# A fused four-block kernel: new order of products and turnings in a projection, and a choice by quarters in a routing

## The reference, cut to what matters

```
h = shift_token(x)                      # x: 2 x 1024 x 128
q, k, v = split(h @ wqkv)               # each 2 x 1024 x 512
q = l2norm(q) * q_scale; k = l2norm(k) * k_scale
q, k = rotary_xpos(q, k)                # cos, sin and a scale by position
o = local_attention(q, k, v)            # windows of 64, looking one window back
x = x + o @ wo                          # then a gated feed-forward
```

```
s = softmax(x @ Wr + br)                # 2048 x 64
fs = where(mask(s), s, 0)               # mask: the best 512 groups of 64 sorted scores
fs = fs / (fs.sum(-1) + 1e-6)
h = silu(x @ Wup + bup) * (x @ Wgate + bgate) * fs
out = h @ Wdown + fs @ bdown
```

## Time and profile before

| what | value |
|---|---|
| time of the runs | 1203.18, 1209.27 and 1210.47 us; median 1209.27 |
| profiled execution | 1206.43 us, span of its instructions 1204.6 us |
| mean granted TensorE clock | 0.968 of full speed |
| busy in the span | PE 1074.0 us (89%), PEld 711.9 (59%), DVE 857.7 (71%), ACT 617.3 (51%), POOL 516.7 (43%) |
| POOL's two operations in the projection | 32 adds of 2364 ns mean, 32 multiplies of 1902 ns |

### The profile page before, as it was taken

One profiled execution on the slowest core, in us unless ns is written; L12 is line 12 of the kernel. 1 busy time (PEld: TensorE's weight loads), 2 busy tenths in 40 slices (PEclk: granted clock), 3 DMA queues, 4 the chain that ended last, 5 costly groups with the idle time before them and its releaser, 6 DMA issues. The chain is left out here.

```text
span 1204.6 us, 29628 instructions
## 1 busy us (share of the span) xinstructions
PE 1074.0 (89%) x11763; PEld 711.9 (59%) x11763; DVE 857.7 (71%) x1539; ACT 617.3 (51%) x1416; POOL 516.7 (43%) x453
## 2 busy tenths in 40 slices
PE   6799999899998879998888999876998999988998
PEld 4588655688553448655446856533665454444897
DVE  5788567787567978544886835797467589998655
ACT  3566455666445669544668924500664357754000
POOL 1476302667207985322996521033344047742200
PEclk9899999999999989999998999999999989988999
DMA  3200000200002210011220000000000011100011
GB/s 85 82 1 2 8 7 18 82 1 2 1 1 62 61 31 3 2 72 35 55 59 7 3 15 15 13 4 4 4 5 3 15 25 18 18 14 1 14 30 53
DMA packets 52791, 28.08 MB, mean 23 GB/s; under 512 B 35474, under 2 KB 46268, under 8 KB 52284
## 3 DMA queue, kind: packets, MB, share of 16 engines
q1 hardware_dynamic: 52668, 26.36, 8.8%
HBM read 17.17 MB, written 1.05 MB: 15 GB/s over the span
## 5 line engine op out<-in xcount | busy, mean ns | idle before, releaser
L363 POOL TENSOR_TENSOR A_pr<-A_pr,A_rs 128x1024 f32<-128x1024 f32 x64 | 121.1, 1894 | 57.0 <-DVE A_rs L430 57.0
L467 ACT ACTIVATE A_pr<-psb,A_nm 128x1024 f32<-128x1024 f32 x64 | 71.1, 1111 | 49.9 <-DVE A_nm L424 49.6
L420 DVE TENSOR_REDUCE A_mx<-psb 128x1 f32<-128x1024 f32 x64 | 78.1, 1220 | 8.3 <-PE psb L376 4.5
L1280 POOL TENSOR_TENSOR F_raw<-F_raw,F_rc 128x1024 f32<-128x1024 f32 x32 | 75.6, 2364 | 16.5 <-DVE F_raw L1350 16.0
L2116 PE MATMUL psb<-M_wd,M_gates 128*128 128x128 f32 x512 | 70.7, 282 | 0.0
L2050 PE MATMUL psb<-XL,M_wu 128*128 128x512 f32 x128 | 69.3, 624 | 1.2 <-ACT M_ST L2174 1.2
L2116 PEld LDWEIGHTS psb<-M_wd,M_gates 128*128 128x128 f32 x512 | 65.6, 195 | 3.9 <-DVE M_gates L2348 2.1
L2053 PE MATMUL psb<-XL,M_wg 128*128 128x512 f32 x128 | 67.5, 609 | 0.0
L2348 DVE TENSOR_TENSOR M_gates<-M_hall,psb 128x512 f32<-128x512 f32 x64 | 43.9, 687 | 33.1 <-PE psb L2111 33.0
L1298 PE MATMUL psb<-F_wqkv,F_hst 128*128 128x512 f32 x128 | 61.3, 601 | 6.2 <-ACT F_hst L1361 4.5
L389 PE MATMUL psb<-ident,A_pr 128*128 128x128 f32 x512 | 66.6, 285 | 0.0
(11 more groups left out here) (396 smaller groups left out, 2974.8 us busy)
## 6 DMA issues: line engine op xcount, KB each, us to landing
F_VS<-F_V SPq DMA_DIRECT2D x62, 128.0 KB, 2.3
F_raw<-in_c_xpos_dram SPq DMA_DIRECT2D x3, 1024.0 KB, 4.8
F_wqkv<-in_L_ffn_wqkv_dram SPq DMA_DIRECT2D x3, 768.0 KB, 7.3
A_w<-in_L_attn_w_dram SPq DMA_DIRECT2D x4, 256.0 KB, 3.6
M_wu<-in_L_ffn_Wup_dram SPq DMA_DIRECT2D x16, 64.0 KB, 2.0
M_wg<-in_L_ffn_Wgate_dram SPq DMA_DIRECT2D x16, 64.0 KB, 2.1
M_wd<-in_L_ffn_Wdown_dram SPq DMA_DIRECT2D x16, 64.0 KB, 1.7
M_sel<-in_c_select_dram SPq DMA_DIRECT2D x16, 64.0 KB, 1.9
```

The source lines that it names most:

```text
L363: pool.tensor_tensor(p, p, rs[:, u % 2:u % 2 + 1].broadcast_to([P, SEQ]), ALU.mult).then_inc(scaled, 1)
L420: dve.tensor_reduce(mx[:, u % 2:u % 2 + 1], sview(u), AX, ALU.max).then_inc(maxed, 1)
L467: act.activation(pr[:, u % NP, :], sview(u), ACT.Exp, bias=nm[:, u % 2:u % 2 + 1], scale=scale, accum_out=su[:, u % 2:u % 2 + 1]).then_inc ...
L1280: pool.tensor_tensor(rs[:, o, :], rs[:, o, :], rc[:, o, :], ALU.add).then_inc(unit, 1)
```

## The change

In the projection `make` is cut in two. It now ends after the query and key products and signals a new semaphore, `paired`; the value product becomes a step `value` of its own, with its wait for `v_kept` and its signal `made`. The order on PE becomes `make(n)`, `turn(n - 3)`, `value(n)`, and one turning is left over after the loop. ACT squares when `paired` comes, then keeps the queries and keys of tile `n - 3`, and only then waits for `made` and keeps the value. DVE's wait for POOL moves from before the sum to behind it. In the routing the choice is written in quarters, one ahead of the remainder that needs it; ACT's rounding waits for its own quarter; and POOL's last four gatings wait for all four remainders.

```diff
@@ -1246,8 +1246,8 @@
-                    g = (loaded, zeroed, staged, made, squared, v_kept, summed, rooted, inv, roped, unit, turned, q_kept, k_kept,
-                         dstep, v_moved) = sems("F1", "loaded zeroed staged made squared v_kept summed rooted inv roped unit "
+                    g = (loaded, zeroed, staged, paired, made, squared, v_kept, summed, rooted, inv, roped, unit, turned, q_kept, k_kept,
+                         dstep, v_moved) = sems("F1", "loaded zeroed staged paired made squared v_kept summed rooted inv roped unit "
                                                 "turned q_kept k_kept dstep v_moved", st)
                     with ExitStack() as sc:
                         hs = XL
@@ -1295,7 +1295,10 @@
                                     pe.wait_ge(roped, n - 1)
                                     pe.wait_ge(squared, n - 1)
                                 for i in range(2):
-                                    pe.matmul(bank[2 * o + i], hst[:, o, :], F_wqkv[:, i * HD:(i + 1) * HD], start=True, stop=True)
+                                    last = pe.matmul(bank[2 * o + i], hst[:, o, :], F_wqkv[:, i * HD:(i + 1) * HD], start=True, stop=True)
+                                last.then_inc(paired, 1)
+
+                            def value(n, o, first):
                                 if not (first and o == 0):
                                     pe.wait_ge(v_kept, n)
                                 pe.matmul(bank[4], hst[:, o, :], F_wqkv[:, 2 * HD:3 * HD], start=True, stop=True).then_inc(made, 1)
@@ -1309,14 +1312,26 @@
                                     last = pe.transpose(psb[:, 5 + i // 4, (i % 4) * P:(i % 4 + 1) * P], rs[:, o, i * P:(i + 1) * P], ident[:])
                                 last.then_inc(turned, 1)
                             make(0, 0, True)
+                            value(0, 0, True)
                             make(1, 1, True)
-                            for o in range(2):
-                                make(2 + o, o, False)
-                                turn(o, o, True)
-                            with pe.Fori(2, HT) as i:
+                            value(1, 1, True)
+                            make(2, 0, False)
+                            value(2, 0, False)
+                            make(3, 1, False)
+                            turn(0, 0, True)
+                            value(3, 1, False)
+                            make(4, 0, False)
+                            turn(1, 1, True)
+                            value(4, 0, False)
+                            make(5, 1, False)
+                            turn(2, 0, False)
+                            value(5, 1, False)
+                            with pe.Fori(3, HT) as i:
                                 for o in range(2):
                                     make(2 * i + o, o, False)
-                                    turn(2 * i + o - 2, o, False)
+                                    turn(2 * i + o - 3, 1 - o, False)
+                                    value(2 * i + o, o, False)
+                            turn(NT - 3, 1, False)
                             for o in range(2):
                                 pe.wait_ge(squared, NT - 1 + o)
                                 pe.wait_ge(roped, NT - 1 + o)
@@ -1330,8 +1345,6 @@
                         def combine(dve):
                             def rope(n, o, first):
                                 dve.wait_ge(squared, n + 1)
-                                if not first:
-                                    dve.wait_ge(unit, 2 * n - 2)
                                 t = n % TPS
                                 sums = psb[:, 7, 2 * HEADS * o:2 * HEADS * (o + 1)]
                                 step = chain(dve, dstep, n)
@@ -1342,6 +1355,8 @@
                                 def factor(s, lo, w):
                                     return tab[:, :, s, ds(t * DH + lo, w)].unsqueeze(2).broadcast_to([P, 2, HEADS, w])
                                 step(dve.tensor_reduce(sums, sq[:, o, :].rearrange("p (h d) -> p h d", d=DH), AX, ALU.add))
+                                if not first:
+                                    dve.wait_ge(unit, 2 * n - 2)
                                 dve.tensor_scalar(rn[:, o, :], sums, 1e-24, None, ALU.max).then_inc(summed, 1)
                                 dve.tensor_tensor(c3, src, factor(0, 0, DH), ALU.mult)
                                 if not first:
@@ -1360,11 +1375,14 @@
                             def stage(n, o):
                                 act.activation(hst[:, o, :], hs[:, ds(n * P, P)], ACT.Copy).then_inc(staged, 1)
-                            def tile(n, o, first, last):
-                                act.wait_ge(made, n + 1)
+                            def tile(n, o, first, last, kept=None):
+                                act.wait_ge(paired, n + 1)
                                 if not first:
                                     act.wait_ge(summed, n - 1)
                                 act.activation(sq[:, o, :], psb[:, 2 * o:2 * o + 2, :].rearrange("p a n -> p (a n)"), ACT.Square).then_inc(squared, 1)
+                                if kept is not None:
+                                    keep(kept)
+                                act.wait_ge(made, n + 1)
                                 act.activation(V[:, ds(n, 1), :, :].rearrange("p o h d -> p (o h d)"), bank[4], ACT.Copy).then_inc(v_kept, 1)
                                 if not last:
                                     stage(n + 2, o)
@@ -1379,16 +1397,14 @@
                             act.wait_ge(zeroed, 1)
                             for o in range(2):
                                 tile(o, o, True, False)
-                            for o in range(2):
-                                tile(2 + o, o, False, False)
-                                keep(o)
+                            tile(2, 0, False, False)
+                            tile(3, 1, False, False, 0)
                             with act.Fori(2, HT - 1) as i:
                                 for o in range(2):
-                                    tile(2 * i + o, o, False, False)
-                                    keep(2 * i + o - 2)
+                                    tile(2 * i + o, o, False, False, 2 * i + o - 3)
                             for o in range(2):
-                                tile(NT - 2 + o, o, False, True)
-                                keep(NT - 4 + o)
+                                tile(NT - 2 + o, o, False, True, NT - 5 + o)
+                            keep(NT - 3)
                             keep(NT - 2)
                             exp(0)
                             keep(NT - 1)
@@ -2187,7 +2203,7 @@
                     for u in range(NU - AFTER, NU):
                         unit(u)
                     for c in range(NCH):
-                        act.wait_ge(chosen, c // 2 + 1)
+                        act.wait_ge(chosen, c + 1)
                         act.activation(FS2[0:E, cs(c)], FSF[:, cs(c)], ACT.Copy).then_inc(split, 1)
                     with act.Fori(1, PAIRS) as i:
                         for o in range(2):
@@ -2215,7 +2231,7 @@
                     for u in range(NU):
                         pool.wait_ge(copied, u + 1)
                         if u == NU - AFTER:
-                            pool.wait_ge(chosen, 2)
+                            pool.wait_ge(rest, NCH)
                         pool.tensor_tensor(hall_of(u), hall_of(u), gate_of(u), ALU.mult).then_inc(joined, 1)
                     pool.wait_ge(joined, NU)
                     pool.wait_ge(xkept, 1)
@@ -2329,13 +2345,15 @@
                                                   op0=ALU.mult, op1=ALU.subtract))
                     step(dve.scalar_tensor_tensor(out=w3, in0=w3, scalar=need[:, 0:1], in1=w2, op0=ALU.is_le, op1=ALU.mult))
                     step(dve.tensor_tensor(w1, w1, w3, ALU.add))
-                    for h in range(2):
-                        r = slice(h * E, (h + 1) * E)
-                        dve.tensor_tensor(FSF[:, h * SEQ:(h + 1) * SEQ], w1[r, :], ST[r, :], ALU.mult).then_inc(chosen, 1)
+                    def choose(c):
+                        r = slice(c // 2 * E, (c // 2 + 1) * E)
+                        dve.tensor_tensor(FSF[:, cs(c)], w1[r, cs(c % 2)], ST[r, cs(c % 2)], ALU.mult).then_inc(chosen, 1)
+                    choose(0)
                     for c in range(NCH):
+                        if c + 1 < NCH:
+                            choose(c + 1)
                         dve.wait_ge(split, c + 1)
-                        if c % 2 == 0:
-                            dve.wait_ge(chosen, c // 2 + 1)
+                        dve.wait_ge(chosen, c + 1)
                         dve.tensor_tensor(FS2[E:P, cs(c)], FSF[:, cs(c)], FS2[0:E, cs(c)], ALU.subtract).then_inc(rest, 1)
                     def pair(i, first):
```

## The result

The kernel after the change takes 1200.49 us at the median of 11 runs (1196.27 to 1205.17); the kernel before, in 11 runs, 1209.27 (1203.18 to 1210.96). The ratio is 0.9937, with a 95% interval of 0.9916 to 0.9957: 5 to 10 us less. The forecast was 1199 (1193 to 1208). The profiled execution of after took 1202.3 us, its span 1200.4, 4.2 us under that of before (1204.6), where the sum of the steps was 8.7.

A forecast was written before the change was run, and what follows sets the result against it. POOL was taken as nearly the bound in the projection, a chain of waits through DVE's remainders and PE in the routing. Projection 5.5, routing 1.5 and clock 1.7 sum to 8.7 us: 1197.7 or 1200.6, forecast 1199, range 1193 to 1208.

The forecast's parts named there:

- First tile: Start of each projection: the square waits only for query and key products, 0.95 us earlier, 1.9 us for two.
- The loop: Projection tiles: value product leaves the path to the square, POOL's 4.30 us a tile decides; 3.6 us gained.
- a ring of 4.19: Projection loop: DVE, next query and key products, turning, DVE again; 4.19 us a tile, under POOL's 4.30; upper end 4.55.
- rival B: Projection loop: PE's ring sets the pace at 4.55 us a tile; gain only 1.5 us, 1206; chance 0.17.
- A: Whole kernel: projection and routing gain as worked out, POOL at its floor in the loop; 1199 us; chance 0.55.
- The end: End of each projection: last key copy, first exponentials and third scores all move with POOL's end; no separate gain.
- Rival E: Tail of each projection also comes out at the full clock, 2 us a layer; 12.7 in all, 1195; chance 0.12.
- F: Path to the next stage is another one and nothing moves; 1207 to 1209 us; chance 0.05.
- C: Projection loop: PE pauses in smaller pieces and its clock falls; slower, 1213 with six or seven such tiles; chance 0.05.
- The routing, contention: End of routing: remainders without POOL's gatings take 0.68 us, so the first down product starts 1.5 us earlier.
- The routing, clock: First down products: a shorter PE pause ahead of the bias products recovers 1.7 us of lower clock; other bound 0.
- D: Routing: moved gatings slow DVE's first four products by 1.0 us each; whole gains 4.7, 1203; chance 0.06.

The follow-up runs named there:

- e5: The changed kernel with PE's turning of three tiles back placed between the query and the key product; 1201.57 us in one execution.
- e3: The changed kernel with PE's value product put back ahead of the turning of three tiles back; 1222.65 us in one execution.
- e4: The changed kernel, but turning the tile two back instead of three, value product still last; 1207.07 us in one execution.
- e6: The changed kernel with POOL's last four gatings waiting for the four quarters of the choice, not the remainders; 1199.39 us in one execution.
- e2: The kernel before with only the routing changed, the projection as before; 1204.84 us, ratio 0.9970.
- e8: The kernel before with twelve warming matmuls instead of six on PE ahead of the first selection; 1207.34 us in one execution.
- e1_again: Second series of the kernel with only the projection changed, routing as before, run beside the full change; 1202.84 us, ratio 0.9953.
- e1_projection_only: The full change with the routing as before, so only the projection is changed; 1198.57 us, ratio 0.9920 to the kernel before.

## Why the prediction was right

*First tile.* 0.95 twice was predicted, 0.86 twice came (from POOL's copy to the first add, 8.19 to 7.33 and 8.18 to 7.32). The square starts 0.11 after the fourth product's end (366.30), not right at it.

*The loop.* 3.6 was predicted, 2.06 + 1.44 = 3.5 came. Part of this agreement is luck. The prediction put all of layer 0's 2.3 us over the floor down to the turning and the value product on the path; 0.92 of it was the one fall of the clock between 373.1 and 376.5, and without that the loop gave back 2.6.

The step behind the number, a ring of 4.19, also failed. Measured it is 4.36: DVE after PE takes 0.14 us and not 0.04 (the row chosen was one of ACT after PE), the hand-over to PE and the products take 1.88 to 1.89 together and not 0.06 + 1.72, the turning 1.04 and not 1.09. The upper bound, 4.55, held. So "the ring runs ahead until the turning waits for POOL" is wrong for this order: the turning starts right behind the products, and late in the loop POOL waits for DVE. In e5, whose ring is shorter, the turning does start 0.05 to 0.07 us behind POOL's end from the third tile of layer 0 on. The loss stays small because the early start gives DVE 0.5 us of lead, which ten tiles use up, and a loop of sixteen is nearly over by then. That is rival B in its mechanism and A in its price: three or four tiles at 0.06, some 0.2 us a layer. In a loop of twice the length the ring would decide (an estimate from the same rows). e3 and e5 show it: longer or shorter ring, later or no waits of POOL.

*The end.* "All of it moves with POOL's end" holds: 7.60 and 7.60 after, 7.51 and 7.68 before. Rival E did not come. The tail did not reach the full clock; from the sixteenth add to the third scores of layer 0 the granted clock was 0.57, lower than the 0.90 of before, with 1.97 us for the sixteenth turning instead of 1.09. Yet that stretch grew by only 0.09 us. F is out.

*C.* The steady stretch stayed at 1.00. The kernel before did show a fall in this loop, at its start, so "the trace does not show that so far in the same loop" holds for the steady stretch alone. The Trainium skill (TensorE: Matmul & The Clock Gate, "A second HAM failure mode: psum-queue depth-cycling") describes the swing; the trace of after does not show it in this loop. That of e4 shows a fall beside a pause of 2.42 us, though the page's mechanism was not tested by it.

*The routing, contention.* 1.5 was predicted, 1.57 came; a remainder at 0.69 us against 0.68. From the first remainder to the first down product it is 7.79 us, where 8.0 was predicted.

*The routing, clock.* 1.7 was predicted, 1.63 came in the profiles. As a term of the median it is smaller: in the old order the clock fell in two of three profiles, so the regained time is about 1.1 us on average, by an estimate from these three. The reading of before was off in a detail: PE did two selections between the warming products and the bias products (1116.27 and 1117.85), not one.

*D* did not come. Two of DVE's products take 1.28 us beside POOL's gatings (1117.76), the same as in the kernel before at 1121.19, where the gatings had ended (1114.31 + 6.30 = 1120.61); the third and fourth of DVE's products, 0.69 us each, had hardly a gating left to meet. The remainder pair in e6, of which a gating held up the second, took 2.36 instead of 1.35. DVE's products read PSUM and SBUF, the remainders SBUF alone. The Trainium skill (SBUF — State Buffer, "Who interferes with whom") says that a DVE instruction contends with a POOL one that reads SBUF when both its inputs are in SBUF, and not with one such input; the traces agree with it on both sides.

*The sum.* The forecast of 1199 lies 1.5 under the median. The sum from the profiled execution alone, 1206.43 - 8.7 = 1197.7, was 4.6 under the profiled 1202.3, by the 4.1 us of the third block. And the 12 us that the prediction took for the least that a measurement can tell was too much: the interval of the ratio, 0.9916 to 0.9957, is 5 us wide and lies clear of 1.

**What stays open.** The third block took 199.7 to 200.4 us in the three profiles with the old projection and 201.6 to 204.8 in the ten with a new one, e3 and e4 among them. The code is the same. Much of the spread goes with the clock: at a mean granted clock of 0.97 in the block (before, e2) it took 200.4 and 199.7 us, at 0.93 (after, e4) 204.5 and 204.8. But at 0.96 it took 199.7 with the old projection (e8) and 201.6 to 202.3 with a new one (four profiles). So some 2 us may go with the change; that the block starts at another time or behind another clock could be the reason, and no run took that apart. Between the totals, the projection alone gained 9.7 and 5.7 us by its two ratios and 5.2 in its stages; the first, 7.0 to 12.2 by its interval, speaks against such a loss, and the second, 3.1 to 8.1, leaves room for it. Whether the new order keeps the clock from falling at the start of a projection, where the old one let it fall in four of six, was not tested by itself either.

## What to carry to other kernels

When a step is moved off one path, add up the ring that it joins with the hand-overs of the very engines in that ring, and compare it with the floor to a few hundredths: a ring 0.06 us over the floor is free for as many tiles as the first tile's lead pays for, then it sets the pace. Where two engines contend over short instructions, let the one that has time wait; splitting the other's work to fit between is then only cost. Compare stages, not whole profiles: an unchanged block moved by 4 us between two executions that were to show 8.

## What the runs showed of the hardware

- PE after DVE takes 0.06 or 0.10 us and DVE after PE 0.14 or 0.15 us in this loop, from the end of one instruction to the start of the other.
- The clock's fall comes after a pause of PE and shows up late: in `e1_again` PE was busy 0.55 us of two at 1112 to 1114, the clock was 1.00 until 1120 and 0.65, then 0.50, behind it. It need not come in each execution: with the same order of work `e1_projection_only`, where the pause was 0.8 us shorter, stayed at 1.00.
- Remainders that alternate with POOL's gatings took 5.73, 6.53, 6.70 and 6.80 us for four in four executions of the same instructions, and 2.49 undisturbed. The spread is the first remainder's, and who came first decides it. It took 0.69 us where it started with the first gating, which then took 1.83 instead of 1.27. Where it started 0.32, 0.14 and 0.06 us behind the gating, it took 1.50, 1.67 and 1.75, that is, it ended 1.81 or 1.82 us after the gating's start each time.
